# A graph network's first sums: the first subtraction of every second batch on GpSimd instead of VectorE

## The reference

```
m = relu(x[src] + edge_attr)                                  # layer 0
x = layernorm(x + (1 + eps) * x + segment_sum(m, dst))
# layer 1: twice x = segment_sum(w * x[dst], src), w from the degrees
# layer 2: twice segment_sum(x[src], dst) @ w_rel + x @ w_root + b
# layer 3: relu(segment_sum(edge_weight * (x @ w)[src], dst) + b)
```

## Time and profile before

| | us |
|---|---|
| Median of three runs | 8579.29 |
| Lowest and highest | 8573.34, 8597.21 |
| Span of the profiled execution, first to last instruction | 8586.9 |
| Its own time | 8597.21, the only one of the three above its span |
| Stretch of the first pass's sums, about 3461 to 4067 | 606 |

### The profile page before, as it was taken

The page is one execution under the profiler, slowest core; times in us unless marked ns, Lnnn a source line. Parts: engine busy times, 40 slices in busy tenths (PEclk is TensorE's granted clock), DMA queues, the critical chain, the costliest instruction groups (busy, mean ns, idle before and its releaser), DMA issues. The chain is left out here.

```text
span 8586.9 us, 220516 instructions
## 1 busy us (share of the span) xinstructions
PE 6442.4 (75%) x65965; PEld 5307.0 (62%) x65965; DVE 6964.6 (81%) x11424; ACT 4628.0 (54%) x13918; POOL 5235.2 (61%) x6131
## 2 busy tenths in 40 slices
PE   8998989999954444999567766766677667677777
PEld 8875666666644444899455655655566546666666
DVE  6666666666655655999989999999898999899996
ACT  0266666666655555544893099119903990399900
POOL 0277777777754444433676577657755776488863
PEclk9966555555555555555779988987799789855597
DMA  9577778763346666444799899979997999566695
GB/s 364 94 221 212 209 208 220 213 184 92 92 136 231 228 232 228 131 122 108 265 335 343 311 323 336 347 260 336 336 347 258 336 335 353 205 230 231 228 340 192
DMA packets 1102379, 2097.87 MB, mean 244 GB/s; under 512 B 392650, under 2 KB 570826, under 8 KB 1101610
## 3 DMA queue, kind: packets, MB, share of 16 engines
q1 hardware_dynamic: 774326, 1166.49, 45.0%
q0 software_dynamic: 224928, 663.45, 20.2%
q10 hardware_dynamic: 102612, 261.44, 9.2%
HBM read 1162.29 MB, written 928.60 MB: 243 GB/s over the span
## 5 line engine op out<-in xcount | busy, mean ns | idle before, releaser
L507 POOL DMA_INDIRECT messages_in_parts<-WORK,goal x1850 | 2001.8, 1082 | 724.0 <-issue 417.4
L483 POOL DMA_INDIRECT edge_rows<-WORK x1664 | 1610.3, 968 | 869.0 <-issue 471.6
L1230 DVE TENSOR_TENSOR WORK<-WORK,psum 128x1024 bf16<-128x1024 uint8 x1480 | 1694.6, 1213 | 178.5 <-DMA WORK<-parts_by_slot 156.0
L692 ACT CAST WORK<-psum 128x432 bf16<-128x432 f32 (+1 forms) x4440 | 1736.9, 566 | 153.5 <-PE psum L938 145.2
L938 PE MATMUL psum<-BIG,WORK 128*128 x11840 | 1245.0, 266 | 760.1 <-DVE WORK L1230 696.5
L532 POOL TENSOR_TENSOR BIG<-BIG,WORK 128x48 f32 x2220 | 1196.1, 539 | 989.7 <-ACT WORK L708 389.3
L938 PEld LDWEIGHTS psum<-BIG,WORK 128*128 128x128 bf16 x11840 | 956.3, 116 | 1048.5 <-issue 1044.0
L1032 DVE TENSOR_TENSOR WORK<-lane_k,slot_part 128x1024 bf16<-128x1024 bf16 x2220 | 1549.0, 730 | 3.9 <-PE psum L938 3.9
L966 PE MATMUL psum<-WORK 128*128 128x144 bf16 x14800 | 1261.1, 236 | 334.6 <-DVE WORK L1032 273.3
L944 PE MATMUL psum<-BIG,WORK 128*128 x17760 | 938.1, 215 | 720.2 <-DVE WORK L1232 700.2
L966 PEld LDWEIGHTS psum<-WORK 128*128 128x128 bf16 x14800 | 1101.7, 147 | 494.3 <-issue 385.2
(11 more groups left out here) (183 smaller groups left out, 9964.1 us busy)
## 6 DMA issues: line engine op xcount, KB each, us to landing
WORK<-messages_in_parts SPq DMA_DIRECT2D x1850, 288.0 KB, 4.5
WORK<-parts_by_slot SPq DMA_DIRECT2D x444, 640.0 KB
messages_in_parts<-BIG ACTq DMA_DIRECT2D x37, 2880.0 KB
WORK<-blocks_by_edge SPq DMA_DIRECT2D x416, 256.0 KB
edge_rows<-BIG ACTq DMA_DIRECT2D x1, 76960.0 KB, 243.1
BIG<-edge_rows SPq DMA_DIRECT2D x74, 1040.0 KB
BIG<-whole_messages SPq DMA_DIRECT2D x370, 193.5 KB, 2.4
whole_messages<-BIG ACTq DMA_DIRECT2D x37, 1920.0 KB
```

The source lines that it names most:

```text
L483: pool.indirect_dma_start(rows_dram, bass.IndirectOffsetOnAxis(ap=at_stage[g][:, j:j + 1], axis=0), row_buf[g][:, j, :], None).then_inc(s_ ...
L507: pool.indirect_dma_start(unit_dram, bass.IndirectOffsetOnAxis(ap=goal[1 - d][:, t:t + 1], axis=0), msg[c].rearrange("p k f -> p (k f)"), ...
L692: act.copy(msg[c][:, 3 * b:3 * b + w, :].rearrange("p k f -> p (k f)"), spread_bank(c, 3 * b)[:, 0:w * W3]).then_inc(s_staged[b], 1)
L1230: m = v.tensor_tensor(SEL[c % GB], part_row[c // GB][:, c % GB, :], here_p.to_broadcast([128, T * K]), ALU.is_equal)
```

## The change

GpSimd makes `take_rest` for every odd t, 185 of the 370 batches, with its own semaphore `s_prest`; VectorE keeps the even ones. VectorE's `take_low` waits for the one or the other. In GpSimd's loop the subtraction of batch t stands ahead of `add_sum(t-4)`. `s_rest` now counts 185 in this pass, so the waits of the sixth pass get another offset.

```diff
+        s_prest = sem("rests_ready_on_gpsimd")
...
+        POOLED = 2
+
+        def rest_before(q):
+            return 0 if q == 0 else BATCHES - BATCHES // POOLED
...
+                def take_rest(t):
+
+                    pool.wait_ge(s_relu, t + 1)
+                    wait_past(pool, s_sum, t - (GB - 1))
+                    pool.tensor_tensor(rest[t % GB], z[t % RING], z_high[t % RING], ALU.subtract).then_inc(s_prest, 1)
+
                 for t in range(BATCHES + LAG):
                     u = t - LAG
+                    if kind == "edge" and t < BATCHES and t % POOLED == POOLED - 1:
+                        take_rest(t)
...
-                    wait_past(act, s_rest, t - RING + 1 + cut_before(q))
+                    wait_past(act, s_rest, t - RING + 1 + rest_before(q))
...
-                    act.wait_ge(s_rest, t + 1 + cut_before(q))
+                    act.wait_ge(s_rest, t + 1 + rest_before(q))
...
-                    dve.wait_ge(s_rest, t + 1 + cut_before(q))
+                    dve.wait_ge(s_rest, t + 1 + rest_before(q))
...
                 def take_low(t):
-                    dve.wait_ge(s_rest, t + 1 + cut_before(q))
+                    if t % POOLED == POOLED - 1:
+                        dve.wait_ge(s_prest, t // POOLED + 1)
+                    else:
+                        dve.wait_ge(s_rest, t - t // POOLED + 1)
                     v.tensor_tensor(z_low[t % GB], rest[t % GB], z_middle[t % GB], ALU.subtract).then_inc(s_low, 1)
...
                 for t in range(BATCHES + 3):
-                    if kind == "edge" and t < BATCHES:
+                    if kind == "edge" and t < BATCHES and t % POOLED != POOLED - 1:
                         take_rest(t)
```

## The result

The changed kernel took 8633.06 us (median of 20 runs) against 8601.74 us of the kernel before (20 runs): 31 us slower by the medians. The ratio on record is 1.0039, 95% interval 1.0026 to 1.0052; that is 34 us. The forecast was 65 us slower, with a range of +16 to +141 us; the measured change lies in it, at about half of the forecast.

A forecast was written before the change was run, and what follows sets the result against it. The prediction took VectorE to bound the stretch. It added +49 us for GpSimd keeping VectorE out and +16 us for the first instruction, +65 on 8579, giving 8644 us, range 8595 to 8720.

The forecast's parts named there:

- The bound: Stretch of the sums: VectorE bounds at 1.638 us a batch; TensorE, about a tenth behind, could reach some 1.50.
- What GpSimd costs VectorE: Each of 185 GpSimd subtractions keeps VectorE out 0.736 us and saves it 0.47: +49 us.
- The first instruction: Start of the stretch: GpSimd's first subtraction takes the first add's 18.44 us, delaying VectorE's low part of batch 1: +16 us.
- the other reading: Start of the stretch: GpSimd is shut out until VectorE pauses, which it would now do at once: +0 us.
- The new wait: VectorE's low part in odd batches waits for GpSimd, which has 3.7 us for its instruction and turn: no cost.
- A: GpSimd's turn in the stretch is short, near the memset's 0.33 us: 8569 us, no change that can be told; chance 0.10.
- B: GpSimd's subtraction costs VectorE no more than an add, or nothing; 1.50 us a batch, 8544 us; chance 0.07.
- C: VectorE's wait for GpSimd in odd batches binds, GpSimd taking over 3.7 us: above 8720 us; chance 0.03.

The follow-up runs named there:

- the subtractions without use: Kernel before, VectorE keeping all its subtractions, plus 185 GpSimd subtractions of the same length for which no engine waits in the stretch; stretch 722.8 us against 605.7.
- the kernel with all 370: Changed kernel with every first subtraction on GpSimd, 370 instead of 185; stretch 664.1 us, 58.4 more than the kernel before.
- subtraction, copy and memset: Kernel before plus 185 useless GpSimd instructions of 384 values with two inputs, one or none; stretch 722.8, 661.9 and 606.05 us.
- The two kernels above: Kernel before with one added VectorE wait at batch 8, or with one useless GpSimd add before VectorE begins; stretches 606.0 and 605.8 us.

## Why the prediction was right, and where it was off

*The bound*: right. VectorE had no idle time before and has none after; when it is relieved, TensorE is next, at 1.456 us a batch, for which the forecast had 1.453 and "some of its gap". The gap of 0.15 us between batches was all waiting.

*What GpSimd costs VectorE*: right in kind, too large in size. The forecast took eight times the add's 0.092 us, 0.736; the subtractions without use measured 0.633, those of all batches 0.631 (half of 3.595 us a pair, less the 3.271 before without its two subtractions, 2 x 0.469). From 48 to 384 elements the price rises by 0.541 us, 1.61 ns an element, and leaves some 0.015 us that does not grow with length. The forecast multiplied that fixed part by eight too; with the measured price the term is 185 x (0.633 - 0.469) = +30 us instead of +49. The lengths belong to two different instructions, but GpSimd's own times have the same slope. With VectorE idle an add takes 0.29 us, and the first subtraction of the kernel with all 370, which ended before VectorE began, took 0.83:

```profile
3456.30 0.83 POOL L544 TENSOR_TENSOR WORK<-BIG 128x384 f32<-128x384 f32 x1 [1.19 <-ACT BIG L715]
```

Either is 0.20 us more than it costs VectorE, so 0.20 us of either instruction cost VectorE nothing. "SBUF — State Buffer" of the Trainium skill, section "SBUF: two separate sides", says that a VectorE instruction with two inputs in SBUF and a GpSimd instruction that reads SBUF shut each other out for the whole instruction. That only reading counts, the 0.633, 0.304 and 0 us of subtraction, copy and memset bear out; of the whole instruction, as the profile shows it, the 0.20 us are to be taken off. By the 2.6 cycles per element in "GPSIMD Engine Reference" of the Trainium skill, section 3.1, VectorE would have lost an estimated 0.83 us; the runs show 1.61 ns an element, 1.9 cycles at 1.2 GHz, in what VectorE loses.

*The first instruction*: this step failed. The forecast put 16 us on "whatever comes first" against the other reading that it named, a GpSimd that is shut out until VectorE pauses. GpSimd's first subtraction took 1.18 us in the changed kernel, and the term was nothing. The two kernels above show that the old 18 us were a lock-out that ended with VectorE's pause. But the other reading was right only in part: it had VectorE pause at once after the change, and VectorE did not wait for this subtraction. It had been idle for 0.04 us ahead of its first low part, the next one-hot was stretched to 1.31 us with no idle time around it, and beside the useless subtractions, for which it does not wait in the stretch, the first one took 1.18 us as well. The argument that decided for the wrong reading, that GpSimd gets in easily later on, is true and remains unexplained. The 6 us of "GPSIMD Engine Reference" of the Trainium skill, section 2.1, are there for code that has just been loaded; no run here shows them.

The two errors, 19 us of price and 16 us of start, went the same way and together make what the forecast was too high by. The range holds without the second: with it gone the forecast would have been +49, with the measured price +30, beside 31.5 in the stretch.

*The new wait*: right. The forecast gave GpSimd 3.7 us for instruction and turn; its result stood ready 2.7 us ahead of the low part, and VectorE's groups have no idle time.

*Rivals*: A needed a turn under 0.52 us; its price came from the memset, which does not collide at all. B asked for a subtraction no dearer than an add, and the stretched low part and one-hot rule it out; its 1.50 us a batch was a little high. The sentence that spoke for it, in "Advanced Engine Details and Errata" of the Trainium skill, section "VectorE Performance Modes" (GpSimd collides with two-port modes), does not cover what the runs show: subtractions of 32-bit values, at 1.08 ns an element, are held up as well. C would have shown idle time on VectorE, and there is none.

## What to carry to other kernels

Work moved from a full VectorE to an idle GpSimd is only worth moving if it costs VectorE less there than at home. Where VectorE's own instructions have two inputs in SBUF, look in the trace for a small GpSimd instruction beside them and at how far VectorE's next start is pushed back; here 1.61 ns an element with two inputs against VectorE's 1.08. Price a longer one from two lengths, since a fixed part does not scale. All VectorE instructions of this stretch have two inputs; whether one with a single input is held up, no run here asks.

## What had not been expected

A write alone on GpSimd is free beside VectorE: 185 memsets of 384 elements left the stretch at 606.05 us. And the 18.4 us of GpSimd's first add, which the forecast charged to whatever comes first, were a lock-out through some 36 VectorE instructions in a row, until VectorE paused; after that the longest add of the stretch took 0.81 us.
